# A perceiver block on one core: key and value projections cut into two row tiles of 64 rows, and the tensor engine's order written for two context tiles

## What is computed

```python
q = layernorm(x) @ Wq.T                       # 64 x 256, 32 heads of 8
k, v = context @ Wk.T, context @ Wv.T         # context: 6272 x 256
q, k = rmsnorm(q), rmsnorm(k)                 # per head of 8 columns
out = softmax(q @ k.T * 8**-0.5) @ v
x = x + out
```

## Time and profile before

| | us |
|---|---|
| median of three executions | 223.77 |
| profiled execution: span from first to last instruction | 219.9 |
| rest of an execution, median less that span | 3.9 |
| PE busy | 203.6 (93%) |
| ACT busy | 147.5 (67%) |
| DVE busy | 129.9 (59%) |
| POOL busy | 106.8 (49%) |
| DMA queue 1, share of 16 engines | 79.1% |

### The profile page before, as it was taken

The page is one execution under the profiler, slowest core; times in us unless marked ns, Lnnn a source line. Parts: engine busy times, 40 slices in busy tenths (PEclk is TensorE's granted clock), DMA queues, the critical chain, the costliest instruction groups (busy, mean ns, idle before and its releaser), DMA issues.

```text
span 219.9 us, 7814 instructions
## 1 busy us (share of the span) xinstructions
PE 203.6 (93%) x2973; PEld 135.4 (62%) x2973; DVE 129.9 (59%) x325; ACT 147.5 (67%) x285; POOL 106.8 (49%) x125
## 2 busy tenths in 40 slices
PE   7676899999999999999999999999878889988993
PEld 2354577777777777777777777777656424463441
DVE  1688548666676776758676675776730522835721
ACT  3456788888888888888888888988789013313230
POOL 4335647748576665867658576665737000000000
PEclk9999999999999999999999999999999999999998
DMA  5429999999889998988979999999999997000000
GB/s 184 122 70 226 174 253 216 149 241 247 222 223 202 208 194 205 227 216 213 198 198 202 221 220 200 255 183 234 147 278 248 289 287 211 28 3 0 0 3 12
DMA packets 66816, 39.63 MB, mean 180 GB/s; under 512 B 54007, under 2 KB 60599, under 8 KB 66799
## 3 DMA queue, kind: packets, MB, share of 16 engines
q1 hardware_dynamic: 66367, 38.95, 79.1%
q10 hardware_dynamic: 432, 0.46, 0.7%
HBM read 26.49 MB, written 0.07 MB: 121 GB/s over the span
## 4 chain that ended last, share of the span: by engine, by line
PE 79%; DMA 7%; DVE 6%; ACT 3%; issue 2%; POOL 2%; ACTq 0%; DVEq 0%
PE ps L787 20%; PE ps L809 13%; PE ps L773 11%; PE ps L815 9%; PE ps L812 9%; PE ps L837 5%; DMA kT<-k 5%; PE ps L927 3%; DMA ctx_f<-ctx_t 2%; PE ps L943 2%; PE ps L888 2%; PE ps L846 1%; PE ps L876 1%; POOL k L357 1%; PE ps L935 1%
## 5 line engine op out<-in xcount | busy, mean ns | idle before, releaser
L409 ACT ACTIVATE room<-ps 128x1024 f32<-128x1024 f32 x98 | 100.2, 1029 | 21.1 <-PE ps L773 21.0
L351 POOL TENSOR_TENSOR ctx_lo<-ctx_f,ctx_hi 128x256 fp32r<-128x256 f32 x49 | 36.0, 734 | 54.6 <-DVE ctx_hi L551 52.2
L787 PE MATMUL ps<-room,v_flat 128*17 128x128 f32 x1568 | 52.3, 274 | 0.0
L809 PE MATMUL ps<-wkv_hi,ctx_hi 128*128 128x512 f32 x98 | 43.7, 446 | 2.6 <-DVE k_n L575 1.5
L787 PEld LDWEIGHTS ps<-room,v_flat 128*17 128x17 f32 x1568 | 38.6, 97 | 5.3 <-ACT room L409 0.3
L583 DVE CAST k<-k_n 128x512 f16<-128x512 f32 x49 | 37.9, 774 | 2.6
L812 PE MATMUL ps<-wkv_lo,ctx_hi 128*128 128x512 f32 x98 | 38.8, 396 | 0.4 <-DVE wkv_lo L502 0.4
L343 POOL TENSOR_TENSOR w_all<-w_all,s_ring 128x1024 f32<-128x1024 f32 x16 | 37.9, 2375 | 0.0
L575 DVE TENSOR_TENSOR k_n<-ps,k_r 128x256 f32<-128x256 f32 x49 | 20.8, 424 | 25.2 <-ACT k_r L435 25.2
L357 POOL TENSOR_TENSOR k<-k_n,k 128x256 f16<-128x256 f32 x49 | 33.1, 675 | 5.0 <-DVE k L583 5.0
L773 PEld LDWEIGHTS ps<-q_blk,kT 48*128 48x128 f16 x784 | 22.1, 94 | 21.7 <-issue 13.5
(11 more groups left out here) (113 smaller groups left out, 123.0 us busy)
## 6 DMA issues: line engine op xcount, KB each, us to landing
w_all<-codes SPq DMA_DIRECT2D x16, 512.0 KB, 4.2
ctx_f<-ctx_t SPq DMA_DIRECT2D x48, 128.0 KB, 2.8
up_sb<-up_w SPq DMA_DIRECT2D x5, 704.0 KB, 10.1
s_ring<-scales SPq DMA_DIRECT2D x12, 256.0 KB, 3.8
s_ring<-wo_scales SPq DMA_DIRECT2D x4, 512.0 KB, 5.4
dn_sb<-down_w SPq DMA_DIRECT2D x5, 352.0 KB
kT<-k SPq DMA_TRANSPOSE x49, 3.7
wkv_f<-xwkv ACTq DMA_DIRECT2D x1, 256.0 KB, 3.2
```

The costliest lines, as they stand in the source:

```text
L351: nc.gpsimd.tensor_tensor(ctx_lo[:, split.slot(2)], ctx_f[:, split.slot(4)], ctx_hi[:, split.slot(2)].bitcast(F32), ALU.subtract).then_inc ...
L409: nc.scalar.activation(probs[:, t.slot(2), half], ps_scores[half].rearrange("p b n -> p (b n)"), ACT.Exp).then_inc(exp_done, 1)
L787: last = nc.tensor.matmul(ps_o[CT * j:CT * j + VW, g * P:(g + 1) * P], v_sb[:, t.slot(8), r], probs[:, t.slot(2), half, at:at + P], start= ...
L809: nc.tensor.matmul(ps_kv[a], ctx_hi[:, a, c], wkv_hi[:, c], start=(c == 0), stop=False)
```

## The change

Each projection is cut by array rows: six matmuls on the rows 0 to 63 of the contraction and six on the rows 64 to 127, each with 512 columns. In one step PE issues the upper halves of tile t+7 alternately with the lower halves of tile t+6, which go to different PSUM banks; a third bank is added (`BANKS`), and a tile's projection is complete one step later than it begins. PE's order is written for two steps: in even steps both score halves, then the projections; in odd steps the first score half, the projections, the second score half, and then all four value halves of tiles t-1 and t. ACT squares after both exponentials in even steps, and in odd steps it takes logarithm and exponential for two tiles at once (64 columns); DVE scales and rounds the keys of two tiles in odd steps. All distances grow (context copy nine tiles ahead, projection seven, keys six), and so do the buffers. To make room, `dn_sb` shares its memory with the values, and its loads wait until the last value product is done. `dequantise` begins at step 2, not 3. In the diff, "..." marks what is left out, removed lines of the old bodies among it.

```diff
-U = 8
-PROJ, KV, TR, PV = 5, 4, 3, -1
-FIRST, LAST = -(PROJ + 1), T - PV
-HEAD = KV
-LOOP0 = 1 - PV
-ITERS = (T - PROJ - 1 - LOOP0) // U
+U = 12
+SPLIT, PROJ, KV, TR = 9, 7, 6, 4
+FIRST, LAST = -SPLIT, T
+HEAD = 6
+LOOP0 = 4
+ITERS = (T - SPLIT - LOOP0) // U
 LOOP1 = LOOP0 + ITERS * U
-LAG = 7
-DEQ0, DEQ = 3, 3
+LAG = 9
+DEQ0, DEQ = 2, 3
+BANKS, VALUES = 3, 12
...
+    def batch(self, plus=0):
+        if self.i is None and self.c < 2:
+            return self.c + 1 + plus if self.c + 1 + plus > 0 else None
+        at = self.c // 2 + 2 + plus
+        if self.i is None:
+            return at if at > 0 else None
+        return self.i * (U // 2) + at
...
-        ctx_hi = sb("ctx_hi", [P, 2, DC, P], F32R)
-        ctx_lo = sb("ctx_lo", [P, 2, DC, P], F32R)
+        ctx_hi = sb("ctx_hi", [P, 4, DC, P], F32R)
+        ctx_lo = sb("ctx_lo", [P, 4, DC, P], F32R)
         k_sq = sb("k_sq", [P, 2, D])
-        k_ss = sb("k_ss", [P, 2, XH])
-        k_ln = sb("k_ln", [P, 2, XH])
-        k_r = sb("k_r", [P, 2, XH])
-        k_n = sb("k_n", [P, 2, D])
+        k_ss = sb("k_ss", [P, 2, 2, XH])
+        k_ln = sb("k_ln", [P, 2, 2, XH])
+        k_r = sb("k_r", [P, 2, 2, XH])
+        k_n = sb("k_n", [P, 4, D])
         k12 = sb("k12", [P, 4, PAIRS, RT], F16)
-        v_flat = sb("v_flat", [P, 8 * PAIRS * VW])
-        v_sb = v_flat[:].rearrange("p (s r v) -> p s r v", s=8, r=PAIRS)
+        late = sb("late", [P, NR * 4 * D])
+        dn_sb = late[0:HC, :].rearrange("p (r a s d) -> p r a s d", r=NR, a=2, s=2)
+        v_sb = late[:, 0:VALUES * PAIRS * VW].rearrange("p (s r v) -> p s r v", s=VALUES, r=PAIRS)
...
-        ps_kv = [ps[:, 4, :], ps[:, 5, :]]
+        ps_kv = [ps[:, 4, :], ps[:, 5, :], ps[:, 7, :]]
...
             for r in range(NR):
                 load_round(r)
+            sp.wait_ge(pv_done, 2 * T)
+            for r in range(NR):
+                load_down(r)
...
-                split, keys = t.ahead(PROJ + 1), t.ahead(TR)
+                split, keys = t.ahead(SPLIT), t.ahead(TR)
...
+            def keys_rms(r, first, last):
+                a = r.slot(4) // 2
+                wait(act, ss_done, r.count(plus=1))
+                nc.scalar.activation(k_ln[:, a, first:last + 1], k_ss[:, a, first:last + 1], ACT.Ln, bias=eps_rms[:],
+                                     scale=1.0 / XD).then_inc(ln_done, 1)
+                wait(act, ln_done, r.batch())
+                wait(act, kn_done, r.count(plus=-3 - last))
+                nc.scalar.activation(k_r[:, a, first:last + 1], k_ln[:, a, first:last + 1], ACT.Exp,
+                                     scale=-0.5).then_inc(r_done, 1)
             def step(t):
+                r = t.ahead(KV)
                 if t.exists():
                     exps(t, 0)
...
+                if t.exists() and not t.is_odd():
                     exps(t, 1)
                 if r.exists():
...
+                    squares(r)
+                    if r.is_first(HEAD):
+                        values_first(r)
+                if t.exists() and t.is_odd():
+                    exps(t, 1)
+                if r.exists() and r.is_first(2):
+                    keys_rms(r, r.c, r.c)
+                elif r.exists() and r.is_odd():
+                    keys_rms(r, 0, 1)
+                elif r.i is None and r.c == T - 1:
+                    keys_rms(r, 0, 0)
+            steps(act, step, {-6: queries_copied, -5: queries_rms})
...
-                    wait(dve, kv_mm, split.count(plus=-1))
+                    wait(dve, kv_mm, split.count(plus=-3))
...
             def step(t):
                 r = t.ahead(KV)
...
+                if r.exists() and r.is_first(HEAD):
+                    keys_summed(r)
                     split_context(t)
...
                 else:
                     split_context(t)
                     if r.exists():
                         keys_summed(r)
                         values_copied(r)
...
+                if r.exists() and (r.is_first(2) or (r.i is None and r.c == T - 1)):
+                    keys_scaled(r)
+                    keys_rounded(r)
+                elif r.exists() and r.is_odd():
+                    for k in (r.ahead(-1), r):
+                        keys_scaled(k)
+                        keys_rounded(k)
+            steps(dve, step, {-6: queries_squared, -5: queries_split, -4: queries_placed})
...
+            def project_halves(j):
+                upper, lower = j, j.ahead(-1)
+                if lower.i is None and lower.c == 0:
+                    lower = Tile(None, -1)
+                if upper.exists():
+                    wait(pe, ctx_hi_done, upper.count(plus=1))
+                    wait(pe, ctx_lo_done, upper.count(plus=1))
+                    wait(pe, v_done, upper.count(plus=1 - BANKS))
+                    wait(pe, kn_done, upper.count(plus=1 - BANKS))
+                terms = [(x, w, c) for x, w in ((ctx_hi, wkv_hi), (ctx_hi, wkv_lo), (ctx_lo, wkv_hi)) for c in range(DC)]
+                for k, (x, w, c) in enumerate(terms):
+                    if upper.exists():
+                        half = nc.tensor.matmul(ps_kv[upper.slot(BANKS)], x[top, upper.slot(4), c], w[top, c],
+                                                start=(k == 0), stop=False, skip_group_check=True)
+                        if k == len(terms) - 1:
+                            half.then_inc(half_mm, 1)
+                    if lower.exists():
+                        if k == 0:
+                            wait(pe, half_mm, lower.count())
+                        last = nc.tensor.matmul(ps_kv[lower.slot(BANKS)], x[low, lower.slot(4), c], w[low, c],
+                                                start=False, stop=(k == len(terms) - 1), skip_group_check=True)
+                if lower.exists():
+                    last.then_inc(kv_mm, 1)
             def step(t):
...
+                j, before = t.ahead(PROJ), t.ahead(-1)
+                if t.exists():
+                    scores(t, 0)
+                if t.exists() and not t.is_odd():
+                    scores(t, 1)
+                if j.i is None and j.c == 0:
+                    project_first(j)
+                elif j.exists() or j.ahead(-1).exists():
+                    project_halves(j)
+                if t.is_odd():
                     if t.exists():
...
+                        scores(t, 1)
+                    for v in (before, t):
+                        for half in range(2):
+                            if v.exists():
+                                values(v, half)
+            steps(pe, step, {-7: queries_mm, -4: queries_turned})
```

More of the change, by code:

```diff
@@ L410, in exps, with squares, values_first @@
                                      ACT.Exp).then_inc(exp_done, 1)
+            def squares(r):
+                wait(act, kv_mm, r.count(plus=1))
+                wait(act, ss_done, r.count(plus=-1))
+                nc.scalar.activation(k_sq[:, r.slot(2)], ps_kv[r.slot(BANKS)][:, 0:D], ACT.Square).then_inc(sq_done, 1)
+            def values_first(r):
+                nc.scalar.activation(
+                    v_sb[:, r.slot(VALUES), :, 0:2 * XD],
+                    ps_kv[r.slot(BANKS)][:, D:2 * D].rearrange("p (r v) -> p r v", v=2 * XD),
+                    ACT.Copy).then_inc(v_done, 1)
@@ L539, in split_context @@
             def split_context(t):
[L540 removed]
+                split = t.ahead(SPLIT)
                 if split.i is None and split.c == 0:
@@ L562, in values_copied @@
                 wait(dve, kv_mm, r.count(plus=1))
-                wait(dve, pv_done, r.count(2, -10))
+                wait(dve, pv_done, r.count(2, -16))
                 if r.i is None and r.c == HEAD:
@@ L790, in values @@
                 last.then_inc(pv_done, 1)
-            def step(t):
-                pv, kv = t.ahead(PV), t.ahead(PROJ)
-                for half in range(2):
-                    if t.exists():
-                        scores(t, half)
-                for half in range(2):
-                    if pv.exists():
-                        values(pv, half)
-                if kv.exists():
-                    wait(pe, ctx_hi_done, kv.count(plus=1))
-                    wait(pe, v_done, kv.count(plus=-1))
-                    wait(pe, kn_done, kv.count(plus=-1))
-                    a = kv.slot(2)
-                    for c in range(DC):
-                        if kv.i is None and kv.c == 0:
-                            pe.wait_ge(ready(f"wkv_hi{c}"), 1)
-                        nc.tensor.matmul(ps_kv[a], ctx_hi[:, a, c], wkv_hi[:, c], start=(c == 0), stop=False)
-                        if kv.i is None and kv.c == 0:
-                            pe.wait_ge(ready(f"wkv_lo{c}"), 1)
-                        nc.tensor.matmul(ps_kv[a], ctx_hi[:, a, c], wkv_lo[:, c], start=False, stop=False)
-                    wait(pe, ctx_lo_done, kv.count(plus=1))
-                    for c in range(DC):
-                        last = nc.tensor.matmul(ps_kv[a], ctx_lo[:, a, c], wkv_hi[:, c], start=False, stop=(c == DC - 1))
```

(13 more changed lines are left out.)

69 lines of the change are left out of this document (26 added, 43 removed).

## The result

The changed kernel took 236.53 us (median of four executions, 233.65 to 239.5), the kernel before 223.85 us (median of four, 222.45 to 224.7, the three given above and one taken beside the changed kernel). The forecast was 221.4 with a range of 214.5 to 230: wrong in sign, and outside the range.

The account below looks back on a forecast made before the run. PE's own order was taken to set the pace, 3.15 us per tile. Filling +5.7, steady -10.2, end -0.35 and odd-step stalls +2.5 summed to -2.35, so 223.8 became 221.4 us, range 214.5 to 230.

Parts of the forecast that it names:

- Steady pair, 5.78 us: PE in the loop: two tiles take 5.78 us against 6.30, giving -10.2 us from tile 2 to tile 42.
- rival D: PE's projections: halves don't run side by side, a pair costs 0.47 us, 56 us more, some 277; chance 0.04.
- saving of four changes of form: PE in the loop: of six changes of matmul form per two tiles two are left, 0.105 and 0.12 us.
- order of two starts: POOL and DVE in the loop: dequantise at 5.6 to 5.9, context copy at 5.9; forecast without a blocked copy.
- Rival A: DVE's odd-step context copy blocked behind dequantise delays the keys: 1.0 us lost seven times, +7.2, 228.6; chance 0.33.
- The argument against it: Context copy on DVE: none of 48 copies ran beside a long POOL instruction, all took 274 to 294 ns.
- Odd steps with a dequantise: DVE in the loop: second tile's scaling stands behind a blocked rounding, PE loses 0.35 us, seven times, +2.5.
- filling, +5.7: Pipeline start: PE projects up to tile 6 before first scores; tile 2's scores at 32.2 against 26.53, give or take 1.5.
- End, 18.4: Tile 42's scores to the copy of the sums, paced by ACT: 18.4 us against 18.75, -0.35.
- the first pair: First pair of steps at the end: 5.3 us, followed by two of 4.95 and 3.2.
- `dn_sb`, loaded later: Five transfers, 1.8 MB, covered by the whole self attention; without that cover some 8.5 us would show.

Follow-up runs that it names:

- oneport: Changed kernel with the context copy written as a reduction over one element, same place in DVE's order: 229.8 us median.
- tiny: Changed kernel with GpSimd's dequantise on 16 of its 1,024 columns, so the result isn't the block's: 229.8 us, 1.025 to 1.041 of the kernel before.
- both: Changed kernel with the context copy behind sum and values, and both tiles' keys scaled before either is rounded: 229.2 us, 1.013 to 1.024 of the kernel before.
- copy_late: Changed kernel with DVE's context copy moved behind the sum of squares and the values' copy in every step: 230.2 us median.
- one_best: Changed kernel with copy as reduction, both keys scaled before rounding, zero matmuls in the filling, values tile by tile from step 44: 218.4 us, 0.979 to 0.987 of before.
- best_pairs: one_best with the changed kernel's own order at the end, values of two tiles in every odd step: 223.7 us, 0.993 to 1.003 of the kernel before.

## Why the prediction was wrong

- **Steady pair, 5.78 us: right.** 5.84 to 5.86 measured. Pairs of half projections start 0.23 us apart, so rival D is refuted; the saving of four changes of form came as priced (0.43 of the 0.52 forecast).
- **Where the sum went wrong.** The spans differ by 15.5 us, where -2.35 was forecast. Of these 17.9 us, 7.5 lie in the loop, 6.2 in the filling, 3.3 at the end and 0.9 behind it. Two steps failed: the order of two starts in the loop, and waits of PE that were priced as time but not as clock.
- **The first failed step is the order of two starts on POOL and DVE**, the context copy of odd steps against the dequantise of even ones. The prediction worked out 5.6 to 5.9 for POOL and 5.9 for the copy, wrote that the order hangs on 0.0 to 0.3 us, and forecast the copy first. POOL was first in all seven, three times by 0.04 us (98.26 and 98.30) and four times by 0.23 (79.18 and 79.41). Rival A's price of 1.0 us was right (6.83 to 6.97, so 0.98 to 1.12 over 5.85), and so was its mechanism (`oneport`); its total of 228.6 adds 7.2 for seven times 1.0, and misses what the clock took. The argument against it had no weight: that no copy had run beside dequantise before says nothing on what happens when one does, and the roundings beside it had shown the blocking at 1.55 us.
- **Odd steps with a dequantise, 0.35 us seven times: nearly nothing in the changed kernel.** The roundings were blocked as forecast (1.27 to 1.44 us), but PE lost some 0.1 (5.93 against 5.84 to 5.86); in `oneport` it lost 0.33 to 0.37. A margin of some tenths at the end of a long sum decided again, and fell the other way.
- **Not seen: the turn of the loop,** 0.23 + 0.23 + 0.06 us at the second turn in `tiny` (6.07, 6.07, 5.90), and 6.10 near tiles 6, 18 and 30 of the changed kernel. The kernel before kept 6.29 across its turns.
- **The second failed step: filling, +5.7, measured +11.9.** At a clock of 1.00 and without zeros it is +5.8 and +6.1 (`both` and copy_late, which change DVE's order alone), so the schedule was counted right; with zeros it is +6.7 at 1.00 (`one_best`). The other 6 us are the clock. The prediction wrote PE's waits down in time but at the price of the upper level, and did not ask what the waits do to the clock.
- **End, 18.4: measured 21.7.** 18.9 where the clock was up (`best_pairs`): the first pair was mis-sized (6.16 for 5.3), the later ones are 4.83 for 4.95. The other 2.8 us are the clock.
- **`dn_sb`, loaded later:** at no cost that can be seen; the rest after the copy is 49.7 against 48.8, and 48.8 in `one_best`.

The sum after the fact: +11.9 (filling) -0.2 (steady) +2.9 (end) +0.9 (rest) = 15.5 us between the spans. That the clock fell in the changed kernel's executions and hardly in those before is measured; that it would fall could not be read from the rows of before, where it was up.

**Open:** why PE waits for turned keys in the first half of copy_late (up to 1.2 us), and for up to 1.6 us with no releaser in the profile in tiny and `both`, and not in `oneport`; and what at the loop's turn holds PE. A branch of 243 ns stands just ahead of it on PE's queue in `one_best`, but the kernel before has branches of 208 to 247 ns at its first four turns too and keeps its period; the cause was not tested.

## What to carry to other kernels

When a schedule leaves margins of a few tenths of a microsecond between two engines that can block each other, price both orders and take the bad one as likely as the good one, or write the operation in a form that can't be blocked (here a reduction, 0.13 us dearer a piece and 5.3 us cheaper in the loop). A deeper software pipeline is paid in idle time of PE at the start and the end, and this idle time costs twice, once as time and again as clock; filling the gaps with zero matmuls took 6 to 7 us off the medians (about 4 by the ratios) and narrowed the spread in both kernels. Where a change is a bundle, cost each part alone: the row tiles were worth 7.1 us in the loop, and the pairwise order at the end lost 3.2.

## What was unexpected in the hardware

- The granted clock fell after waits of PE of about 2 us in the filling (0.72 in the mean of 18 to 28 us), and how often it did varied between executions of the same kernel: copy_late ran from 227.4 to 237.4 us with mean clocks of 0.998 to 0.928. In its profiled execution PE had the same waits (2.28, 2.17 and 1.68 us) and the clock stayed at 1.00, so such waits don't always bring a fall; the fall between 8 and 12 us came in kernels with and without zeros, and what decides it isn't known. The Trainium skill (TensorE: Matmul & The Clock Gate, HAM oscillation — how this bites in real kernels) describes such a fall when the engine waits again and again for transferred data; the trace agrees as far as three falls of the filling stand behind waits (2.28, 2.18 and 1.68 us), though these were waits for other engines' results. Taking those gaps away was worth 7 us of 225 in the median. From 18 to 28 us of copy_late (clock is the third number from the end):

```profile
18.00:28.00 10.00, 6.15 (x60) 4.85 (x59) 5.87 (x15) 4.97 (x12) 5.23 (x8) 1.00 0.77 128
```

- One transposing transfer holds SP's queue for 1.23 us at least and 3.46 at most, and lands after 2.7 to 7.7 us (copy_late):

```profile
L295 SPq DMA_TRANSPOSE kT<-k x49: 1231/1262/3456, 19.2 to 165.4; - x49
DMA to landing us min/median/max: 2.7/4.5/7.7
```
